# Routing logits worked out inside the second cross attention, weighing from rows turned back, and a gather-scatter program one slot shallower

## Chip, cores, metric

The kernel runs on one core of one Trainium2 chip. The metric is the device time of one execution in microseconds (us), given as the median of several runs.

## The reference, cut to what matters

Six sublayers work on x, 2 x 1024 tokens of 256 values. The change lies at the seam between the last two:

```python
# second cross attention (16 heads of 16, 64 context positions, a mask), post-norm
x = _layernorm(x + _L1_xattn_ref(x, ctx, ctx, mask, Wk, bk, Wv, bv, Wo, bo))
# experts, post-norm around them
xn = (x - mean(x)) * rsqrt(var(x) + 1e-5) * gamma + beta      # a second normalisation, with gain and offset
logits = clip(xn @ router_w.T, -1e4, 1e4)                     # 2048 x 8
probs = softmax(logits);  top 2 of the 8 experts per token, with their probabilities as gates
out = sum over the two experts of  (silu(g) * u) @ down.T,    g, u = split((gate * xn) @ gate_up.T)
x = _layernorm(x + (x + out))
```

So the router reads a layer norm (with gamma and beta) of a value that is itself a layer norm (without them), and what the experts read is xn times the gate.

## The kernel before, in words

Tokens are cut into TILES = 16 tiles of P = 128 rows. `core.x_nat` holds x by rows (128 x 16 x 256), `core.x_tr` holds it transposed (features on the partitions). PSUM is eight banks: `ps_s` and `ps_e` are two each, `ps_q`, `ps_c`, `ps_ct` and `ps_y` one each; `ps_ct` is idle in the cross attention.

**Stages.** `decoder` runs the sublayers as stages. Each is an `nc.Block()` with one program for each engine, written out in order by hand; semaphores join them, and a stage begins when every engine has left the one before. `core.stage()` then clears its semaphores.

**The second cross attention** (`stage_cross_attention`, `cross_attention`). A software pipeline over tiles: in step s an engine works on tile s (queries), s-1 (scores), s-2 (exponential and row sums), s-3 (weights, transposed), s-4 (mixing, output product, residual, moments) and s-5 (normalised row written). CROSS_LAGS = 5, so there are 21 steps. In one step TensorE does, in this order: mask and scores (L846, L854), mixing (L868), queries (L879), output product (L886), transposes of the weights (L893). ScalarE does the exponential (L902), `mixed_tr` (L907), the queries' bias (L913), the normalised row `x_nat` (L917), `e_tr` (L925). GpSimd multiplies by 1/sum (L822), turns the variance into rstd and offset (L826, L828, L830) and adds x and bias (L833). VectorE takes the maxima, subtracts, sums (L932 to L942) and makes z and its moments (L947 to L952). The sync engine (SP) starts the loads of the experts' weights (`following.load`).

**The experts' front** (first part of `stage_experts`). VectorE takes moments of all 16 tiles of x_nat (L2508, L2511), GpSimd rstd (L2297), VectorE subtracts, scales and multiplies by the gamma row (L2519, L2522), GpSimd adds the beta row into `xn`, which lies in x_tr's room (L2302). TensorE transposes xn two tiles at a time (L2354), ScalarE copies that out of PSUM (L2442), TensorE makes the logits (L2363). Then VectorE alone works out softmax, the two picks, each token's slot and the expert of each slot tile (L2529 to L2605). Meanwhile ScalarE has written 2x into `doubled` (L2431), which SP stores as the sums' start value `summed_rows` (L2252, L2254); once the gates are there ScalarE writes gate times xn for both picks (L2453, 32 of them), which SP stores as `gated_rows` (L2259), and GpSimd waits for that store and for the source index before it gathers.

**The split of the down weights.** fp32 products are made of three rounded ones, so every expert's down matrix is split: the high part by ScalarE (L2434, `split_high`), the low part by VectorE (L2236, `split_low`). Before, ScalarE does four in the front and four after `gated_written`; VectorE does four in the front and two in each of the first two steps of the loop.

**The experts' loop.** 39 slot tiles, software-pipelined by `lagged(engine, count, depth, step)`: in turn g GpSimd gathers tile g (L2218) and scatters, adding into `summed_rows`, a tile of some turns ago (L2321). Before, that is tile g-4. TensorE: hidden transposes (L2392), gate-up product (L2402), row transposes (L2409), down product (L2420), in that order, the down product two tiles behind. ScalarE copies the output out (L2492). A scatter waits until the one before it has landed. The last part loads the sums, normalises and stores.

```python
if g is not None and not at(g, 0):
    need(pool, rows_tr_ready, g - 1); pool.wait_ge(gathered, 16 * g); fetch(pool, g, turn)
if u3 is not None:
    pool.wait_ge(down_copied, u3 + 1); need(pool, scattered, 16 * u3)
    nc.gpsimd.indirect_dma_start(summed_rows, ..., rows_out[turn % UNROLL], None, compute_op=ALU.add)
```

Of the kernel before, what the change touches and what calls it, by code (L numbers as in the profile page):

```python
# [758 lines left out]

CROSS_LAGS = 5  # L760
# [3 lines left out]
def cross_attention(core, ctx, layer, weights, setup):  # L764
# [31 lines left out]
    var_eps, rstd, offset = (core.sb(ctx, f"{pre}_{n}", [P, 1]) for n in ("var_eps", "rstd", "offset"))  # L796
# [20 lines left out]
    def pool_step(pool, step):  # L817
# [5 lines left out]
        if u5 is not None:  # L823
            pool.wait_ge(var_ready, u5 + 1)
            need(pool, xn_ready, u5)
            nc.gpsimd.tensor_scalar(var_eps[:], mv[:, 1:2], LN_EPS, None, ALU.add).then_inc(eps_added, 1)  # L826
# [3 lines left out]
            nc.gpsimd.tensor_scalar(offset[:], mv[:, 0:1], rstd[:, 0:1], -1.0, ALU.mult, ALU.mult).then_inc(offset_ready, 1)  # L830
# [4 lines left out]
    def pe_step(pe, step):  # L835
# [37 lines left out]
        if t is not None:  # L873
# [7 lines left out]
            last.then_inc(q_ready, 1)  # L881
        if u4 is not None:
# [13 lines left out]
    def act_step(act, step):  # L896
# [18 lines left out]
        if u5 is not None:  # L915
            act.wait_ge(offset_ready, u5 + 1)
            nc.scalar.activation(x_nat[:, u5, :], z[:], ACT.Identity, bias=offset[:, 0:1],  # L917
                                 scale=rstd[:, 0:1]).then_inc(xn_ready, 1)
        if u3 is not None:
# [39 lines left out]
def stage_cross_attention(core, layer, weights, setup, following):  # L959

    nc = core.nc
    with core.stage() as ctx:
        cross = cross_attention(core, ctx, layer, weights, setup)
        with nc.Block() as block:

            @block.sync
            def _(sp):
                following.load(sp)

            @block.gpsimd  # L970
            def _(pool):
                for step in range(CROSS_STEPS):
                    cross.pool_step(pool, step)

            @block.tensor
            def _(pe):
                for step in range(CROSS_STEPS):
# [3 lines left out]
            def _(act):  # L981
                for step in range(CROSS_STEPS):
# [3 lines left out]
            def _(dve):  # L986
                setup.dve_keys(dve)
                setup.dve_values(dve)
                for step in range(CROSS_STEPS):
# [1105 lines left out]
def stage_experts(core, weights):  # L2095
# [9 lines left out]
    xn = core.x_tr[:].rearrange("p k (h d) -> p (k h) d", d=D)  # L2105
# [5 lines left out]
    BATCHED = BANK // D  # L2111
# [5 lines left out]
    with core.stage() as ctx:  # L2117
        scratch = core.shared[:].rearrange("p (t d) -> p t d", d=D)
        router = core.sb(ctx, "ex_router", [P, KD, EXPERTS])
# [30 lines left out]
        gamma_row, beta_row = (core.sb(front_ctx, f"ex_{n}_row", [P, D]) for n in ("gamma", "beta"))  # L2150
# [3 lines left out]
        xn_tr = [core.sb(front_ctx, f"ex_xn_tr{i}", [P, BATCHED, KD, P]) for i in range(2)]  # L2154
# [7 lines left out]
        KEPT = EXPERTS // 2  # L2162
# [589 lines left out]
```

## Time and profile before

| | us |
|---|---|
| median of 3 runs (1361.65 to 1364.32) | 1362.62 |
| the profiled execution | 1365.14 |
| its span, first to last instruction | 1363.4 |
| second cross attention, first to last TensorE instruction of it | 973.25 to 1071.65 |
| first VectorE instruction of the experts' stage | 1075.94 |
| VectorE reads the logits | 1110.27 |
| first gather issued | 1133.99 |
| last scatter issued | 1340.24 |

Times inside the trace are counted from the span's start. The rows shown further down come from the trace's views; an engine's rows give the start, the duration, the engine, the line, the operation, output<-input, and in brackets the idle time before it and what ended it. PE is TensorE's matmul side, PEld its weight load, DVE VectorE, ACT ScalarE, POOL GpSimd, SP the sync engine. PE's durations overlap one another (a matmul's end is modelled), so the distance between starts is what to read.

### The profile page before, as it was taken

What the parts mean: (1) busy time and instruction counts of PE and PEld (TensorE: products, weight loads), DVE (VectorE), ACT (ScalarE), POOL (GpSimd) and SP (SyncE); (2) the same over time, 40 slices, a digit from 0 to 9 for tenths busy, and PEclk for the clock granted to TensorE, in tenths of its full rate; (3) what the DMA queues carried; (4) which work ended last, traced back from release to release, by engine and by line L of the source; (5) the groups of instructions that cost most, each with busy time, mean ns of one, the idle gap of its engine ahead of it and who ended that gap; (6) DMA issues with size and microseconds to landing.
All of it is one profiled execution on the core that took longest, in us unless ns stands there. A gap on an engine that the chain in (4) does not pass through costs nothing. (4 is left out here: it accounts for less than half of the span.)

```text
span 1363.4 us, 25768 instructions
## 1 busy us (share of the span) xinstructions
PE 1176.5 (86%) x8215; PEld 872.0 (64%) x8216; DVE 871.6 (64%) x1536; ACT 789.9 (58%) x2129; POOL 599.9 (44%) x618
## 2 busy tenths in 40 slices
PE   7888589677799999999989999999799356999991
PEld 3544367455566777777666677767577254888881
DVE  2488789874245555566345556666588687888883
ACT  2488547423556655566455556665266355777773
POOL 1155437646454421530353232210166524888873
PEclk9999889887699999999999999999999756999996
DMA  9100000000110000000110000100460221333334
GB/s 300 44 1 1 0 1 1 1 16 16 28 36 17 16 17 16 17 17 1 32 32 16 17 1 17 47 1 2 163 209 1 74 92 55 53 54 55 55 50 135
DMA packets 42138, 58.29 MB, mean 43 GB/s; under 512 B 6608, under 2 KB 34640, under 8 KB 42032
## 3 DMA queue, kind: packets, MB, share of 16 engines
q1 hardware_dynamic: 34544, 46.70, 11.4%
q0 software_dynamic: 7488, 10.23, 4.7%
q8 instruction: 60, 0.98, 0.3%
q14 instruction: 46, 0.38, 0.1%
HBM read 32.80 MB, written 13.63 MB: 34 GB/s over the span
## 5 line engine op out<-in xcount | busy, mean ns | idle before, releaser
L2021 DVE TENSOR_REDUCE ga_neg_top<-ps 128x1 f32<-128x128 f32 (+7 forms) x256 | 182.0, 752 | 194.5 <-PE ps L1791 194.1
L1911 ACT COPY ga_e_tr<-ps 128x512 f32<-128x512 f32 (+3 forms) x192 | 92.1, 479 | 174.6 <-PE ps L1800 171.9
L1902 ACT ACTIVATE ga_e<-ps,ga_neg_top 128x128 f32<-128x128 f32 (+7 forms) x256 | 188.2, 743 | 7.5 <-DVE ga_neg_top L2021 6.8
L1800 PE MATMUL ps<-ident,ga_e 128*128 128x128 f32 x1152 | 165.1, 279 | 0.8 <-DVE ga_e_tr L2029 0.8
L1816 PE MATMUL ps<-ga_e_tr,ga_v 128*64 128x256 f32 x1152 | 151.7, 391 | 4.1 <-ACT ga_att L1919 4.1
L1800 PEld LDWEIGHTS ps<-ident,ga_e 128*128 128x128 f32 x1152 | 123.3, 142 | 28.0 <-ACT ga_e L1902 14.7
L2029 DVE COPY ga_e_tr<-ps 128x128 f32<-128x128 f32 (+3 forms) x192 | 105.8, 551 | 35.1 <-PE ps L1800 34.8
L2613 DVE TENSOR_TENSOR ex_w_lo<-ex_gate_up,ex_w_hi 128x1024 fp32r<-128x1024 f32 x78 | 95.5, 1225 | 35.1 <-ACT ex_w_hi L2467 32.1
L1976 POOL TENSOR_TENSOR ga_q_lo<-shared,ga_q_hi 128x1024 fp32r<-128x1024 f32 x15 | 35.5, 2369 | 174.7 <-ACT ga_q_hi L1892 174.7
L1816 PEld LDWEIGHTS ps<-ga_e_tr,ga_v 128*64 128x64 f32 x1152 | 72.4, 136 | 49.0 <-issue 23.4
L822 POOL TENSOR_TENSOR xa_e<-xa_e,xa_recip 128x1024 f32<-128x1024 f32 x32 | 60.9, 1902 | 68.7 <-DVE xa_recip L942 68.7
L2467 ACT CAST ex_w_hi<-ex_gate_up 128x1024 fp32r x78 | 81.6, 1049 | 15.6 <-issue 13.0
L1788 PE MATMUL ps<-ga_k_hi,ga_q_hi 64*128 64x512 f32 (+3 forms) x384 | 79.3, 409 | 4.1 <-PEq L162 2.3
L497 ACT ACTIVATE ca_e<-ps,ca_neg_top 128x64 f32<-128x64 f32 x256 | 75.9, 361 | 0.2 <-DVE ca_neg_top L528 0.2
L1962 POOL TENSOR_TENSOR shared<-shared,ga_cos 128x1024 f32<-128x1024 f32 x18 | 42.6, 2368 | 74.8 <-DMA shared<-shared 72.0
L2321 POOL DMA_INDIRECT summed_rows<-shared,ex_tile_target x39 | 62.5, 1603 | 20.7 <-issue 9.0
L1251 PE MATMUL ps<-x_tr,wide_weights 128*128 128x128 f32 x512 | 68.6, 291 | 2.0 <-ACT ga_e_tr L1911 2.0
L1251 PEld LDWEIGHTS ps<-x_tr,wide_weights 128*128 128x128 f32 x512 | 64.2, 204 | 8.2 <-issue 5.8
L1788 PE MATMUL ps<-ga_k_lo,ga_q_hi 64*128 64x512 f32 (+3 forms) x384 | 67.7, 348 | 0.0
L1788 PE MATMUL ps<-ga_k_hi,ga_q_lo 64*128 64x512 f32 (+3 forms) x384 | 67.6, 348 | 0.0
L497 ACT ACTIVATION_READ_ACCUMULATOR ca_e<-ps,ca_neg_top 128x1 f32 x256 | 65.1, 255 | 0.0
L1301 ACT ACTIVATE shared<-ps,ga_bq 128x128 f32<-128x128 f32 x128 | 36.5, 368 | 45.7 <-PE ps L1251 43.6
(335 smaller groups left out, 2830.8 us busy)
## 6 DMA issues: line engine op xcount, KB each, us to landing
shared<-shared SPq DMA_DIRECT2D x80, 128.0 KB, 2.4
ex_gate_up<-in_ex_gate_up SPq DMA_DIRECT2D x1, 8192.0 KB, 24.2
ex_down<-in_ex_down SPq DMA_DIRECT2D x1, 4096.0 KB, 35.8
x_tr<-in_x_tr SPq DMA_DIRECT2D x4, 512.0 KB, 7.0
x_nat<-in_x SPq DMA_DIRECT2D x1, 2048.0 KB, 11.4
gated_rows<-shared SPq DMA_DIRECT2D x8, 256.0 KB, 2.2
gated_rows<-x_tr SPq DMA_DIRECT2D x8, 256.0 KB, 2.3
x_tr<-summed_rows SPq DMA_DIRECT2D x8, 256.0 KB, 5.3
```

The source lines that it names most:

```text
L497: last = nc.scalar.activation(e[buffer][:, keys], ps_scores[buffer][:, keys], ACT.Exp, scale=SCALE, bias=neg_top[buffer][:, m:m + 1], accu ...
L1251: last = nc.tensor.matmul(bank[:, g * P:(g + 1) * P], wq[:, k, block_of], x_tr[:, k, J * P:(J + 1) * P], start=(k == 0), stop=(k == KD - 1))
L1788: nc.tensor.matmul(ps_scores(t, half)[:, k0:k1], qs[J % 2][rows, c * R + r, :], ks[slot][rows, c, 0:k1 - k0], start=(i == 0), stop=(i == 2 ...
L1800: last = nc.tensor.transpose(ps_tr[n % 2][:, (kb - k0) * P:(kb - k0 + 1) * P], e[half][t % 2][:, kb * P:(kb + 1) * P], core.ident[:])
L1816: last = nc.tensor.matmul(ps_att[half * HD:(half + 1) * HD, :], v[:, v_slot(b, kb), kv * HD:(kv + 1) * HD], e_tr[g % 2][:, kb, half, :], s ...
L1902: nc.scalar.activation(e[half][t % 2][:, 0:blocks(t) * P], ps_scores(t, half), ACT.Exp, bias=neg_top[t % 2][:, half:half + 1], accum_out=s ...
L1911: nc.scalar.copy(e_tr[g % 2][:, k0:k1, half, t % 2 * P:(t % 2 + 1) * P], ps_tr[n % 2][:, 0:(k1 - k0) * P].rearrange("p (k t) -> p k t", t= ...
L2021: nc.vector.tensor_reduce(neg_top[t % 2][:, half:half + 1], ps_scores(t, half), AX.X, ALU.max, negate=True).then_inc(top_ready, 1)
L2029: nc.vector.tensor_copy(e_tr[g % 2][:, k0:k1, half, t % 2 * P:(t % 2 + 1) * P], ps_tr[n % 2][:, 0:(k1 - k0) * P].rearrange("p (k t) -> p k ...
L2321: nc.gpsimd.indirect_dma_start(summed_rows, bass.IndirectOffsetOnAxis(ap=tile_target[turn % UNROLL][:], axis=0), rows_out[turn % UNROLL], ...
L2467: nc.scalar.copy(w_hi[buffer][:, k, :], weights.gate_up[:, bass.ds(x, 1), k, :] .rearrange("p a n -> p (a n)")).then_inc(w_hi_ready, 1)
L2613: nc.vector.tensor_tensor(w_lo[buffer][:, k, :], weights.gate_up[:, bass.ds(x, 1), k, :].rearrange("p a n -> p (a n)"), w_hi[buffer][:, k, ...
```

## The change

1. A new class `Router` works inside the second cross attention, which runs 23 steps in place of 21. For tile s-5, GpSimd works out a second rstd and offset beside the first (the norm of a norm: rstd of var(1+eps)+eps^2), and ScalarE writes the doubly normalised row, without gamma and beta, into `scaled`. For tile s-6 TensorE transposes it and ScalarE writes it into x_tr with gamma and beta, now one value for each partition. For tile s-7 TensorE makes the logits in `ps_ct`. The router's three small loads come ahead of the experts' weights on SP.
2. The front of the experts' stage loses its normalisation, transposes and logits. VectorE begins with the clip of the logits.
3. TensorE turns x_tr back to rows in PSUM, four tiles at a time (`turn_back`), and ScalarE weighs them from there into `scratch` (first pick) and into `doubled`'s room (second pick), in the order WEIGHED; `gated_rows` is stored in 8 pieces in place of 16.
4. ScalarE's doubling comes behind its exponential. The down weights: ScalarE splits four behind the weighing and two in each of the loop's first two steps; VectorE two before the loop (AHEAD = 2) and three in each of the first two steps.
5. GpSimd's program of the loop: depth 3 in place of 4, so turn g gathers tile g and scatters tile g-3.

```diff
+class Router:
+    def pe_step(self, pe, step):
+        u5, u6, u7 = self.tiles_of(step)
+        if u7 is not None:
+            pe.wait_ge(self.moved, u7 + 1)
...
+            for k in range(KD):
+                last = nc.tensor.matmul(self.logits[:, u7 * EXPERTS:(u7 + 1) * EXPERTS], self.xn_tr[:, k, u7 * P:(u7 + 1) * P],
+                                        self.router[:, k, :], start=(k == 0), stop=(k == KD - 1))
+            last.then_inc(self.routed, 1)
+        if u6 is not None:
+            pe.wait_ge(self.scaled_ready, u6 + 1)
+            need(pe, self.moved, u6)
+            for k in range(KD):
+                last = nc.tensor.transpose(self.ps_xn[:, k * P:(k + 1) * P], self.scaled[u6 % 2][:, k * P:(k + 1) * P], self.core.ident[:])
+            last.then_inc(self.turned, 1)
+    def act_scale(self, act, u, z, offset, rstd):
+        need(act, self.turned, u - 1)
+        return self.core.nc.scalar.activation(self.scaled[u % 2][:], z, ACT.Identity, bias=offset, scale=rstd).then_inc(self.scaled_ready, 1)
+    def act_step(self, act, step):
...
+            act.wait_ge(self.turned, u6 + 1)
+            for k in range(KD):
+                last = nc.scalar.activation(self.xn_tr[:, k, u6 * P:(u6 + 1) * P], self.ps_xn[:, k * P:(k + 1) * P], ACT.Identity,
+                                            bias=self.beta[:, k:k + 1], scale=self.gamma[:, k:k + 1])
+            last.then_inc(self.moved, 1)
...
+            if router is not None:
+                nc.gpsimd.tensor_scalar(var_eps[:, 1:2], mv[:, 1:2], 1.0 + LN_EPS, LN_EPS * LN_EPS, ALU.mult, ALU.add)
-            nc.gpsimd.tensor_tensor(rstd[:], var_eps[:], core.neg_half[:], ALU.pow).then_inc(rstd_ready, 1)
+            nc.gpsimd.tensor_tensor(rstd[:], var_eps[:], core.neg_half[:].to_broadcast([P, NORMS]), ALU.pow).then_inc(rstd_ready, 1)
...
+                def turn_back(n):
+                    if n >= 2:
+                        pe.wait_ge(gated_ready, WEIGHED.index((n - 2, 1)) + 1)
+                    for i in range(BANKED):
+                        for k in range(KD):
+                            columns = slice((n * BANKED + i) * P, (n * BANKED + i + 1) * P)
+                            last = nc.tensor.transpose(ps_xn[n % 2][:, (i * KD + k) * P:(i * KD + k + 1) * P], core.x_tr[:, k, columns], core.ident[:])
+                    last.then_inc(xn_ready, 1)
...
+                for n, i in WEIGHED:
+                    if n == 0:
+                        act.wait_ge(gates_ready, i + 1)
+                    if n == 0 and i == 1:
+                        act.wait_ge(summed_written, 16 * (TILES // DOUBLED + 1))
+                    if i == 0:
+                        act.wait_ge(xn_ready, n + 1)
+                    for j in range(BANKED):
+                        t = n * BANKED + j
+                        last = nc.scalar.activation(gated(i, t, 1).rearrange("p a d -> p (a d)"), ps_xn[n % 2][:, j * D:(j + 1) * D],
+                                                    ACT.Copy, scale=gates[:, i, t:t + 1])
+                    last.then_inc(gated_ready, 1)
+                for x in range(KEPT):
                     split_high(x)
+                act.wait_ge(gated_written, 16 * 2 * TILES // BANKED)
...
-                lagged(pool, SLOT_TILES, 4, step, turns=True)
+                lagged(pool, SLOT_TILES, 3, step, turns=True)
```

WEIGHED is (0,0), (1,0), (0,1), (1,1), (2,0), (2,1), (3,0), (3,1) as (group of four tiles, pick).

## Rows read from the trace of the kernel before

**Rows 1.** The page: shares of the chain that ended last, by engine.

```profile
DMA 7%; issue 4%; POOL 3%; DVE 1%; PE 1%; POOLq 0%; ACT 0%; DVEq 0%; ACTq 0%
```

**Rows 2.** Stretches: us, busy time of each engine (instructions), clock, DMA share, GB/s.

```profile
1000.00:1060.00 60.00, 59.02 (x525) 45.78 (x523) 52.56 (x78) 38.94 (x77) 40.06 (x55) 1.00 0.14 45
1160.00:1320.00 160.00, 160.00 (x991) 141.30 (x990) 131.02 (x166) 122.72 (x198) 131.69 (x133) 1.00 0.34 54
```

**Rows 3.** Timeline of the experts' front, VectorE.

```profile
1075.94 5.32 DVE L2508 BATCH_NORM_STATS2 ex_stats<-x_nat 128x6 f32<-128x256 f32 x16 [3.16 <-PEq L162]
...
1110.27 0.29 DVE L2529 TENSOR_SCALAR ex_logits<-ps 128x128 f32<-128x128 f32 x1 [0.43 <-PE ps L2363]
...
1112.98 0.29 DVE L2542 TENSOR_REDUCE ex_gates<-ex_probs 128x16 f32<-128x128 f32 x1
...
1132.55 0.18 DVE L2601 TENSOR_SCALAR ex_source<-ex_choice 128x40 int32<-128x40 int32 x1
```

**Rows 4.** Timeline of one steady step of the cross attention, TensorE.

```profile
1032.63 1.17 PE L846 MATMUL ps<-xa_mask_parts,xa_ident 128*128 128x512 f32 x4
...
1034.80 0.64 PE L868 MATMUL ps<-xa_e_tr,shared 128*32 128x128 f32 x16
1035.37 1.16 PE L879 MATMUL ps<-x_tr,wide_weights 128*128 128x128 f32 x8
1036.37 1.03 PE L886 MATMUL ps<-wide_weights,xa_mixed_tr 128*128 128x256 f32 x4
1037.23 1.04 PE L893 MATMUL ps<-ident,xa_e 128*128 128x128 f32 x8
1038.03 1.17 PE L846 MATMUL ps<-xa_mask_parts,xa_ident 128*128 128x512 f32 x4
```

**Rows 5.** The same step on ScalarE.

```profile
1032.48 1.08 ACT L925 COPY xa_e_tr<-ps 128x512 f32<-128x512 f32 x2 [0.19 <-PE ps L893]
1035.59 0.37 ACT L907 COPY xa_mixed_tr<-ps 128x256 f32<-128x256 f32 x1 [1.08 <-PE ps L868]
1036.57 0.63 ACT L913 ACTIVATE xa_q_tr<-ps,xa_bq 128x128 f32<-128x128 f32 x2 [0.61 <-PE ps L879]
1037.08 0.60 ACT L917 ACTIVATE x_nat<-xa_z,xa_offset,xa_rstd 128x256 f32<-128x256 f32 x1
```

**Rows 6.** The last step of the cross attention, ScalarE.

```profile
1074.15 0.60 ACT L917 ACTIVATE x_nat<-xa_z,xa_offset,xa_rstd 128x256 f32<-128x256 f32 x1 [2.74 <-POOL xa_offset L830]
```

**Rows 7.** The front: doubling, weighing, and the stores' landing (last number, us).

```profile
1077.83 1.99 ACT L2431 ACTIVATE ex_doubled<-x_nat 128x1024 f32<-128x1024 f32 x2
1119.82 6.47 ACT L2453 ACTIVATE x_tr<-x_tr,ex_gates 128x256 f32<-128x256 f32 x16
gated_rows<-x_tr SPq DMA_DIRECT2D x8, 256.0 KB, 2.3
summed_rows<-wide_weights SPq DMA_DIRECT2D x1, 128.0 KB, 4.5
```

**Rows 8.** First steps of the experts' loop, VectorE and TensorE.

```profile
1140.81 2.36 DVE L2236 TENSOR_TENSOR ex_down_rounded<-ex_down,x_rounded 128x1024 fp32r<-128x1024 f32 x2
1150.83 0.92 PE L2420 MATMUL ps<-x_rounded,shared_rounded 128*128 x4 [2.07 <-DVE shared_rounded L2619]
```

**Rows 9.** GpSimd and ScalarE around the loop's scatters: steady and last.

```profile
1236.24 1.01 POOL L2218 DMA_INDIRECT shared<-gated_rows,ex_tile_source  x1 [0.72 <-POOL ex_tile_target L2212]
1236.93 0.37 ACT L2492 COPY shared<-ps 128x256 f32<-128x256 f32 x1
1238.61 1.61 POOL L2321 DMA_INDIRECT summed_rows<-shared,ex_tile_target  x1 [0.17 <-issue]
1241.06 1.01 POOL L2218 DMA_INDIRECT shared<-gated_rows,ex_tile_source  x1 [0.65 <-POOL ex_tile_target L2212]
...
1340.24 1.57 POOL L2321 DMA_INDIRECT summed_rows<-shared,ex_tile_target  x1 [2.85 <-DMA summed_rows<-shared,ex_tile_target]
```

**Rows 10.** The chain that ended last, first piece of the loop.

```profile
1133.99 3.01 DMA shared<-gated_rows,ex_tile_source
```

More of the change, by code:

```diff
@@ L881, in pe_step @@
             last.then_inc(q_ready, 1)
+        if router is not None:
+            router.pe_step(pe, step)
         if u4 is not None:
@@ L962, in stage_cross_attention @@
     with core.stage() as ctx:
-        cross = cross_attention(core, ctx, layer, weights, setup)
+        router = Router(core, ctx)
+        cross = cross_attention(core, ctx, layer, weights, setup, router)
+        steps = TILES + Router.LAGS
         with nc.Block() as block:
@@ L971, in _ @@
             def _(pool):
-                for step in range(CROSS_STEPS):
+                for step in range(steps):
                     cross.pool_step(pool, step)
@@ L976, in _ @@
             def _(pe):
-                for step in range(CROSS_STEPS):
+                for step in range(steps):
                     cross.pe_step(pe, step)
@@ L981, in _ @@
             def _(act):
-                for step in range(CROSS_STEPS):
+                for step in range(steps):
                     cross.act_step(act, step)
@@ L988, in _ @@
                 setup.dve_values(dve)
-                for step in range(CROSS_STEPS):
+                for step in range(steps):
                     cross.dve_step(dve, step)
@@ L2104, in stage_experts @@
     nc, dram = core.nc, core.dram
-    xn = core.x_tr[:].rearrange("p k (h d) -> p (k h) d", d=D)
+    sums = core.x_tr[:].rearrange("p k (h d) -> p (k h) d", d=D)
     ROUTES = TILES * EXPERTS
@@ L2109, in stage_experts @@
     GROUP = 2
-    BATCHED = BANK // D
+    BANKED = 2 * (BANK // D)
+    WEIGHED = [(0, 0), (1, 0), (0, 1), (1, 1)] + [(n, i) for n in range(2, TILES // BANKED) for i in range(2)]
     LEFT = EXPERTS // 2
@@ L2254, in _ @@
                 sp.dma_start(summed_rows[N:N + P, :], doubled[0][:, 0, :]).then_inc(summed_written, 16)
[L2255 to L2260 removed]
+                for turn, (n, i) in enumerate(WEIGHED):
+                    tiles = slice(n * BANKED, (n + 1) * BANKED)
+                    sp.wait_ge(gated_ready, turn + 1)
+                    sp.dma_start(gated_rows[i * N:(i + 1) * N, :].rearrange("(n p) d -> p n d", p=P)[:, tiles, :],
+                                 gated(i, n * BANKED, BANKED)).then_inc(gated_written, 16)
                 sp.wait_ge(scattered, 16 * SLOT_TILES)
@@ L2308, in _, with step @@
                 fetch(pool, 0, 0)
-                def step(g, t, u1, u2, u3, turn):
+                def step(g, t, u1, u2, turn):
                     if g is not None and not at(g, 0):
@@ L2487, in step @@
                         weights_high(ahead, 0, turn % 2)
+                    if at(t, 0) or at(t, 1):
+                        first = KEPT + t * (EXPERTS - KEPT) // 2
+                        for x in range(first, first + (EXPERTS - KEPT) // 2):
+                            split_high(x)
                     if u2 is not None:
@@ L2607, in _ @@
                 dve.wait_ge(weights.loaded, 16 * weights.LOADS)
+                for x in range(AHEAD):
+                    split_low(dve, x, down_first_ready)
                 def weights_low(t, k, buffer):
@@ L2635, in step @@
                     if at(t, 0) or at(t, 1):
-                        first = KEPT + t * (EXPERTS - KEPT) // 2
-                        for x in range(first, first + (EXPERTS - KEPT) // 2):
+                        first = AHEAD + t * (EXPERTS - AHEAD) // 2
+                        for x in range(first, first + (EXPERTS - AHEAD) // 2):
                             split_low(dve, x, down_lo_ready)
```

172 lines of the change are left out of this document (66 added, 106 removed).

## The prediction

> **What bounds the kernel now.** I read the page's chain of waits first: its shares name the scatter's DMA and the issue time around it [rows 1], so the chain hardly tells what lies ahead of the loop; for that I took stretches and timelines. Stretches show three regimes. In the steady cross attention TensorE is busy 59.02 of 60 us; in the steady loop 160.00 of 160, at a granted clock of 1.00 (2.4 GHz) in both [rows 2]. Between them the experts' front is one serial line: VectorE starts at 1075.94, reads the logits only at 1110.27, and has the source index at 1132.55 [rows 3]. Call the moment at which VectorE reads the logits T; all that follows hangs on it: gates at T+3.0, sources at T+22.5, first gather at 1133.99 = T+23.7 [rows 3, 10]. Nothing overlaps that line, so what shortens it shortens the kernel, less what is put into the two TensorE-bound regimes.
>
> **1. The front's normalisation and logits go.** VectorE's first instruction of the stage becomes the read of the logits: 1110.27 - 1075.94 = -34.3 us [rows 3]. What was hidden beneath these 34 us (doubling, four splits high and low, the masks, the start values' store) has to find another cover; parts 4 and 5 charge for it.
>
> **2. TensorE in the steady cross attention.** Its groups follow each other without a gap, one step from 1032.63 to 1038.03 = 5.4 us [rows 4]. Router adds four instructions of 128x128 weights: two transposes and two products of 8 columns. Eight query products take 1036.37 - 1035.37 = 1.00 us, or 0.125 each; eight transposes 1038.03 - 1037.23 = 0.80, or 0.10 each. So 2 x 0.125 + 2 x 0.10 = 0.45 us a step. Steps 6 to 15, ten of them, are bound so (the pipeline has five lags, and queries end at step 15), the first with transposes only: 10 x 0.45 - 0.1 = +4.4 us. The new waits are met a step ahead: `scaled` and x_tr's tile are written by ScalarE in the step before. Bounds: 0 if gaps of TensorE's sequencer take them in; 10 x 1.1 = 11 if each new semaphore costs a visible gap.
> By the Trainium skill, "TensorE: Matmul & The Clock Gate", section Back-to-back issue gap, a stream of weight loads and matmuls sustains about 81 ns for each at 128 columns. The rows show 100 to 125 ns for these fp32 forms; by the page the part would be an estimated 10 x 0.32 = 3.2 us. The measured spacing stands.
>
> ScalarE gets three more a step: the scaled row, like L917's 0.60, and two copies out of PSUM, like L913's two in 0.63: 1.23 us. It stands idle 1.08 before L907, 0.61 before L913 and 0.19 before L925, 1.88 together [rows 5]. `e_tr` ended at 1033.56, and TensorE's mixing began at 1034.80 [rows 4, 5]: 1.24 of slack, plus the 0.45 by which TensorE comes later. I charge nothing. GpSimd gets one small tensor_scalar and a wider power, 0.35 us as I estimate it (0.2 for the first, 0.1 to 0.15 for the second); it stands idle by a third (40.06 busy of 60) [rows 2].
>
> **3. Two more steps at the end.** In the last steps TensorE isn't full and the order is a chain through GpSimd and ScalarE. GpSimd's +0.35 falls on it three times (tiles 13, 14, 15): +1.0. ScalarE's extra work of step 18 stands once ahead of the last `e_tr`: +1.2 at most; I take 1.1, with both copies. Then the last scaled row starts where x_nat did at 1074.15 [rows 6] and, in place of x_nat's end at 1074.75, there come: the scaled row 0.6 (x_nat now runs beside what follows), two transposes 0.3, two copies 0.7, two products 0.4, handovers 0.4 = 2.4 against 0.6, +1.8. Sum +3.9; bounds 2 and 7 (each handover doubled, clock at its lower level).
>
> **4. Doubling and weighing ahead of the gather.** ScalarE's line from T: exponential done T+1.3; doubling 4 x 0.97 [rows 7] to T+5.2; gates are there by T+3.1. Weighing is 32 x 0.405 = 13.0 (6.47 for 16 [rows 7]), read from PSUM now. The second pick must wait for the store of 2x, which is its room. Before, these stores started at 1077.6 and the last (issue to landing 4.5 us [rows 7]) was in near 1085.3, 7.7 later; now they start at T+2.4, so T+10.1. (0,0) and (1,0) are done at T+8.5: a stall of 1.6. Then (0,1) to T+11.8; TensorE turns group 2 back until T+13.8 (8 transposes at half clock, some 1.8), (1,1) done T+13.4, so 0.5 of stall; the other four groups to T+20.3. The last store is half a megabyte: landing 2.3 for 256 KB [rows 7], which I raise to 2.9; gated_written at T+23.3, against sources at T+22.5: the gather starts 0.8 later. Splits high 0 to 3 (3.9 us) hold ScalarE until T+24.2, which delays the first high weights by about the same 0.8. +0.8; bounds 0 and 4 (the start values' store twice as late as I have it).
> The Trainium skill, "DMA: Bandwidth & Descriptors", section Anatomy of one DMA, gives about 2.0 us plus bytes at 436 GB/s; an estimate from it for half a megabyte is 3.2, and the part would be +1.1. No row of before shows this size alone.
>
> **5. The splits inside the loop.** VectorE does three low splits in each of steps 0 and 1 where it did two (2.36 for two, 1.18 each [rows 8]). In both steps VectorE is what TensorE waits for: the first down product came at 1150.83 after 2.07 idle, released by VectorE [rows 8]. 2 x 1.18 = 2.4, of which 0.7 goes where VectorE itself waited for ScalarE's high weights: +1.7. Bounds 0 and 3.5 (ScalarE's four in the same steps in series too).
>
> **6. GpSimd three deep.** In the steady loop TensorE is full; GpSimd repeats every 4.82 (1236.24 to 1241.06), and a scatter starts 1.31 after ScalarE's copy (1237.30 to 1238.61) since the gather of the same turn stands ahead of it [rows 9]. With depth 3 that gather is past already: scatter 0.9 after the copy, -0.4, kept only until the scatters run one behind the other at the end, and then handed through to the last (1340.24). The gather of tile g now comes after the scatter of g-4: copy 0.37, 0.9, 2.45 to the gather (1238.61 to 1241.06), landing L, transposes and down product 2.1: 5.8 + L within two tiles, 9.64. L is 3.01 unloaded [rows 10]; in the steady loop the next gather was released by GpSimd's own copy and not by its landing, so L is below 1240.4 - 1236.24 = 4.2 [rows 9]. So -0.4; bounds -0.8 and, at L = 4.2, (10.0 - 9.64) / 2 x 36 = +6.5.
>
> **Sum.** -34.3 + 4.4 + 3.9 + 0.8 + 1.7 - 0.4 = -23.9 us. The profiled execution took 1365.14 (span 1363.4 and 1.74 around it) and becomes 1341.2; the median, 2.5 lower, becomes 1338.7.
>
> **Rivals.**
> *A. ScalarE becomes the cross attention's bound.* Its new work stands between queries and `e_tr`. If its 1.23 came in series with TensorE rather than beside it: 12.3 in place of 4.4, 1346.6. For it: the copies wait for transposes that TensorE now does after the queries. Against: the 1.88 us of idle time and the 1.24 of slack.
> *B. The gather binds the loop.* From L = 3.85 on. At 4.2: 1338.7 + 6.9 = 1345.6. Against: 3.01 in the one clear row; for: that row has no scatter beside it.
> *C. Better than summed.* TensorE's 0.45 vanishes in gaps and the first steps' splits are covered by waits: 1338.7 - 4.4 - 1.7 = 1332.6.
> *D. Slower than before.* One mechanism: in turn g the gather of the next tile stands behind a scatter that itself waits for the landing of the one before, and TensorE waits for the gather. The loop then closes on GpSimd. It costs all 23.9 us from 23.9 / 36 = 0.66 a tile, that is L = 3.85 + 2 x 0.66 = 5.2, above the 4.2 that the trace allows, unless the new order makes the two DMAs collide. 1364 and more.
> *E. The logits don't come earlier as said*, since the weighing hides none of the stores: the start values' store late by 4 more, 1342.7.
>
> **Chances.** Forecast (1335 to 1342) 0.52; A 0.16; B 0.08; C 0.12; E 0.08; D 0.03; 0.01 for no change. 0.2% of the time, 2.7 us, is about what a measurement tells from none. Faster 0.96, same 0.01, slower 0.03. The range runs from C's neighbourhood to beyond A: 1332 to 1349.
>
> **What would show it.** VectorE's read of the logits at 1075.9 + 8.3 = 1084 to 1085; steady steps of the cross attention 5.85 in place of 5.4, TensorE without gaps; ScalarE's last weighing 20.3 after the logits; first gather 24.5 after them; first down product 43 after them (40.6 before); 4.8 a tile in the loop, and the scatter 0.9 behind the copy. Wrong would be: VectorE's read later than 1090, steady steps of 6.5 or more, TensorE waiting for a gather in the loop, or a first gather more than 28 after the logits.

## The result and the profile after

The changed kernel takes 1348.32 us in the median of four runs (1348.17 to 1351.78), the kernel before 1363.47 in the runs beside it (1361.65 to 1364.44): a ratio of 0.9897, 95% interval 0.9877 to 0.9916. Faster by 15.2 us, where 23.9 was forecast. The time lies inside the range given (1332 to 1349), but 9.6 above the forecast itself and outside the 1335 to 1342 around it.

Both traces cut at the same events give the sum term by term. The events are the first VectorE instruction of the second cross attention, its fifth and its sixteenth row maximum (the last one), VectorE's read of the logits (T), the first gather, and the first down product and last scatter of the loop. All are starts, in us.

| stretch | before | after | difference | forecast |
|---|---|---|---|---|
| first VectorE instruction to fifth maximum | 23.86 | 23.83 | 0.0 | 0 |
| fifth to sixteenth maximum | 59.33 | 65.19 | +5.9 | +4.4 (part 2) |
| sixteenth maximum to T, without the 34.33 of the old front | 19.42 | 30.79 | +11.4 | +3.9 (part 3) |
| the old front | 34.33 | 0 | -34.3 | -34.3 (part 1) |
| T to first gather | 23.72 | 26.14 | +2.4 | +0.8 (part 4) |
| first gather to first down product | 16.84 | 18.50 | +1.7 | +1.7 (part 5) |
| first down product to last scatter | 189.41 | 189.72 | +0.3 | -0.4 (part 6) |
| last scatter to the end | 23.16 | 22.71 | -0.5 | 0 |
| sum | 390.07 | 376.88 | -13.2 | -23.9 |

The spans differ by 16.8 (1363.4 and 1346.6): the stretch began at 973.33 before and at 969.72 after. Nothing ahead of it was changed, and over the fourteen traces of this study it began anywhere from 969.72 to 973.93, so 3.6 of the 16.8 is no gain of the change.

The regimes of [rows 2], the same stretches of the kernel after:

```profile
1000.00:1060.00 60.00, 60.00 (x540) 48.18 (x540) 47.37 (x71) 45.97 (x100) 40.64 (x61) 1.00 0.11 33
1160.00:1320.00 160.00, 158.30 (x975) 138.96 (x974) 124.94 (x158) 117.85 (x191) 104.59 (x127) 1.00 0.33 52
```

The cross attention is TensorE's still. In the loop TensorE is not quite full any more: 158.30 in place of 160.00, and 975 instructions in place of 991.

VectorE's timeline of the front, where [rows 3] stood: the logits, the first gates, the sources.

```profile
1089.53 0.29 DVE L2561 TENSOR_SCALAR ex_logits<-ps 128x128 f32<-128x128 f32 x1 [8.31 <-PEq L162]
...
1092.25 0.29 DVE L2574 TENSOR_REDUCE ex_gates<-ex_probs 128x16 f32<-128x128 f32 x1
...
1111.82 0.18 DVE L2633 TENSOR_SCALAR ex_source<-ex_choice 128x40 int32<-128x40 int32 x1
```

From T to the sources it is 22.29, as before (22.28). T itself is 1089.53, and 1084 to 1085 was forecast.

One steady step of the cross attention on TensorE, for [rows 4]:

```profile
1032.35 1.18 PE L912 MATMUL ps<-xa_mask_parts,xa_ident 128*128 128x512 f32 x4
...
1035.09 1.16 PE L945 MATMUL ps<-x_tr,wide_weights 128*128 128x128 f32 x8
1036.09 0.51 PE L794 MATMUL ps<-ro_router,x_tr 128*128 128x8 f32 x4
1036.45 0.42 PE L801 MATMUL ps<-ident,ro_scaled 128*128 128x128 f32 x2
1036.71 1.03 PE L954 MATMUL ps<-wide_weights,xa_mixed_tr 128*128 128x256 f32 x4
```

The router's share is 1036.71 - 1036.09 = 0.62: the products 0.36 as *four* instructions, the transposes 0.26 as two.

ScalarE in the same step, for [rows 5]:

```profile
1030.78 0.60 ACT L807 ACTIVATE ro_scaled<-xa_z,xa_offset,xa_rstd 128x256 f32<-128x256 f32 x1
1031.27 0.59 ACT L987 ACTIVATE x_nat<-xa_z,xa_offset,xa_rstd 128x256 f32<-128x256 f32 x1
1031.77 0.80 ACT L817 ACTIVATE x_tr<-ps,ro_beta,ro_gamma 128x128 f32<-128x128 f32 x2
1032.45 1.07 ACT L997 COPY xa_e_tr<-ps 128x512 f32<-128x512 f32 x2
```

`e_tr` starts at 1032.45 and is needed by the mixing at 1034.52: here the new work is covered, as argued. Rival A, which ended at 1346.6, is not what happened: no steady step took 6.5, they took 6.02 where 5.85 was forecast.

The last steps on TensorE:

```profile
1065.35 1.04 PE L961 MATMUL ps<-ident,xa_e 128*128 128x128 f32 x8
1069.18 1.08 PE L934 MATMUL ps<-xa_e_tr,shared 128*32 128x128 f32 x16 [2.80 <-ACT xa_e_tr L997]
...
1071.53 1.91 PE L954 MATMUL ps<-wide_weights,xa_mixed_tr 128*128 128x256 f32 x4
1073.24 1.92 PE L961 MATMUL ps<-ident,xa_e 128*128 128x128 f32 x8
...
1084.83 1.02 PE L794 MATMUL ps<-ro_router,x_tr 128*128 128x8 f32 x4 [3.57 <-ACT x_tr L817]
```

and the same time in stretches (TensorE's busy time first, the granted clock third from the end):

```profile
1066.00:1069.00 3.00, 0.39 (x4) 0.14 (x2) 1.03 (x3) 2.61 (x6) 2.83 (x4) 1.00 0.00 0
1069.00:1070.00 1.00, 0.82 (x16) 0.60 (x16) 0.00 (x0) 0.13 (x1) 0.85 (x3) 0.56 0.00 0
1070.00:1072.00 2.00, 2.00 (x16) 1.72 (x9) 0.00 (x0) 1.58 (x4) 1.21 (x3) 0.50 0.03 8
```

TensorE waited 2.80 for ScalarE's `e_tr`. As that wait ended the granted clock went from 1.00 to 0.50 (2.4 to 1.2 GHz), and it was 0.50 until the router's end. The output product (L954) shows what that costs: 1.71 from start to start, where a steady step has 0.86. The kernel before had a wait at the same place, a shorter one:

```profile
1065.36 0.64 PE L868 MATMUL ps<-xa_e_tr,shared 128*32 128x128 f32 x16 [1.82 <-ACT xa_e_tr L925]
```

Its clock was 1.00 up to 1076, behind the end of this stage.

The stores of T to the first gather. Columns as above, DMA share and GB/s last:

```profile
1093.00:1095.00 2.00, 0.17 (x1) 0.00 (x0) 1.70 (x6) 1.91 (x3) 0.00 (x0) 0.99 1.02 341
...
1099.00:1101.00 2.00, 0.00 (x0) 0.00 (x0) 1.77 (x7) 1.15 (x4) 0.00 (x0) 0.50 1.02 340
...
1111.00:1113.00 2.00, 0.00 (x0) 0.00 (x0) 1.83 (x9) 2.00 (x3) 0.00 (x0) 0.50 0.56 206
```

The landing of the stores, for [rows 7], and ScalarE's stall in the weighing:

```profile
gated_rows<-shared SPq DMA_DIRECT2D x4, 512.0 KB, 4.5
```
```profile
1099.85 3.02 ACT L2505 ACTIVATE wide_weights<-ps,ex_gates 128x256 f32<-128x256 f32 x8 [2.14 <-DMA summed_rows<-wide_weights]
```

GpSimd at the end of them, where the first gather of [rows 10] stood:

```profile
1113.73 1.00 POOL L2286 COPY ex_tile_source<-ex_source 128x1 int32<-128x1 int32 x1 [22.90 <-DMA gated_rows<-ex_doubled]
1115.67 1.24 POOL L2295 DMA_INDIRECT shared<-gated_rows,ex_tile_source  x1 [0.94 <-POOL ex_tile_source L2286]
```

and at the same time the issue of the last store, and VectorE's two low splits ahead of the loop:

```profile
1109.44 0.36 SPq L2332 DMA_DIRECT2D gated_rows<-ex_doubled  x1
```
```profile
1112.33 2.35 DVE L2313 TENSOR_TENSOR ex_down_rounded<-ex_down,x_rounded 128x1024 fp32r<-128x1024 f32 x2
```

From the first store (1093) the 16 DMA engines are taken, at some 340 GB/s, but for one gap. The sources are there at 1111.82, and what GpSimd waits for until 1113.73 is the last store. Then its copy of one column takes 1.00, where the same copy took 0.18 in the kernel before (at 1132.87). It ends at 1114.73, 0.05 behind the second of the two splits.
By the Trainium skill, "DMA: Bandwidth & Descriptors", section Anatomy of one DMA, which is about transfers that GpSimd issues (these are SP's), bytes move at 436 GB/s. By that figure the 6.4 MB of these stores are an estimated 14.7 us. At the measured 340 GB/s they are 18.9, and the measurement decides.

The first steps of the loop, for [rows 8]: three low splits of VectorE, and the first down product.

```profile
1129.36 3.49 DVE L2313 TENSOR_TENSOR ex_down_rounded<-ex_down,x_rounded 128x1024 fp32r<-128x1024 f32 x3
```
```profile
1134.17 0.72 PE L2476 MATMUL ps<-x_rounded,shared_rounded 128*128 x4
```

GpSimd in the steady loop, for [rows 9], and after it what GpSimd waited for from 1160 to 1300 (us in total, times, longest):

```profile
1171.43 1.71 POOL L2385 DMA_INDIRECT summed_rows<-shared,ex_tile_target  x1 [1.40 <-ACT shared L2547]
1172.56 1.17 POOL L2289 COPY ex_tile_target<-ex_target 128x1 int32 x1
1173.88 1.01 POOL L2295 DMA_INDIRECT shared<-gated_rows,ex_tile_source  x1 [0.15 <-POOL ex_tile_target L2289]
```
```profile
POOL summed_rows L2385 <- ACT shared L2547: 16.0, 12, 1.5
POOL summed_rows L2385 <- DMA summed_rows<-shared,ex_tile_target: 15.1, 11, 1.6
POOL summed_rows L2385 <- DMA shared<-gated_rows,ex_tile_source: 10.2, 6, 1.7
```

ScalarE's copy of that tile ran from 1170.19 for 0.37, so the scatter starts 0.87 behind the copy's end, as forecast (0.9; before 1.31 [rows 9]).

### The profile page after: what moved, and what is told of

Its sections match the earlier page's. It is cut to its first block and busy times, and to the rows that moved or that the text cites. A ratio compares the mean times of both kernels' runs of the same rounds, so it can differ in the third digit from the quotient of the medians.

```text
span 1346.6 us, 25817 instructions
## 1 busy us (share of the span) xinstructions
PE 1181.1 (88%) x8247; PEld 874.8 (65%) x8248; DVE 845.7 (63%) x1479; ACT 802.1 (60%) x2169; POOL 567.5 (42%) x625
## 3 DMA queue, kind: packets, MB, share of 16 engines
q1 hardware_dynamic: 34672, 46.44, 11.4%
## 5 line engine op out<-in xcount | busy, mean ns | idle before, releaser
L1875 PEld LDWEIGHTS ps<-ident,ga_e 128*128 128x128 f32 x1152 | 123.3, 142 | 28.0 <-ACT ga_e L1977 14.7
```

What stands on the lines that cost most here:

```text
L1875: last = nc.tensor.transpose(ps_tr[n % 2][:, (kb - k0) * P:(kb - k0 + 1) * P], e[half][t % 2][:, kb * P:(kb + 1) * P], core.ident[:])
```

## The experiments

Each kernel starts from the changed one unless it says otherwise. "Way" is from the last maximum to T; the columns behind the ratio are from one traced execution of each kernel. Kernels with the same figure under "before" were timed beside the same runs of the kernel before. The edits are shown cut, and their comments say where a line was or went.

| kernel | median us (runs) | before | ratio, 95% | way | T to gather | gather to down | down to last scatter |
|---|---|---|---|---|---|---|---|
| e1_depth4 | 1348.76 (4) | 1362.71 | 0.9905, 0.9889 to 0.9922 | 28.91 | 26.13 | 18.04 | 188.76 |
| e2_warm | 1346.97 (4) | 1362.71 | 0.9879, 0.9859 to 0.9900 | 29.23 | 26.12 | 18.05 | 190.82 |
| e3_behind | 1346.04 (4) | 1362.71 | 0.9870, 0.9847 to 0.9894 | 26.69 | 25.69 | 18.02 | 190.25 |
| e4_warm_behind | 1345.90 (4) | 1362.71 | 0.9879, 0.9861 to 0.9896 | 25.82 | 24.99 | 18.07 | 191.21 |
| e5_twin_z | 1344.57 (4) | 1364.01 | 0.9855, 0.9839 to 0.9872 | 25.81 | 26.14 | 18.05 | 189.75 |
| e6_copies_first | 1344.73 (4) | 1364.01 | 0.9859, 0.9842 to 0.9875 | 25.21 | 26.14 | 18.01 | 189.52 |
| e7_few_start_values | 1346.03 (4) | 1364.01 | 0.9877, 0.9861 to 0.9894 | 30.82 | 23.73 | 18.28 | 189.47 |
| e8_double_first | 1346.53 (4) | 1364.01 | 0.9876, 0.9860 to 0.9893 | 28.89 | 25.00 | 18.06 | 189.58 |
| e9_joined | 1344.29 (5) | 1362.47 | 0.9870, 0.9854 to 0.9885 | 25.23 | 25.01 | 18.10 | 189.90 |
| e11_vector_weights | 1344.37 (5) | 1362.47 | 0.9869, 0.9854 to 0.9885 | 28.65 | 24.99 | 18.12 | 189.10 |
| e10_vector_weights_depth3 | 1345.53 (5) | 1362.47 | 0.9874, 0.9858 to 0.9891 | 28.64 | 25.00 | 18.11 | 190.93 |
| e12_changed_again | 1350.18 (6) | 1362.47 | 0.9908, 0.9892 to 0.9924 | 30.78 | 26.14 | 18.50 | 189.60 |

**e1_depth4: GpSimd's depth alone put back.**

```diff
-lagged(pool, SLOT_TILES, 3, step, turns=True)
+lagged(pool, SLOT_TILES, 4, step, turns=True)
```

> The changed kernel with GpSimd's program of the loop four deep again, everything else as changed. Theory: TensorE is the bound of the loop at either depth (4.85 us a tile in the changed kernel too), so the depth is worth nothing but where the last scatters stand: 1348.3 + 0.4, within 0.2%. Rival (the gather binds the shallower loop): faster by 1.5 us or more, with the time between the first down product and the last scatter shrinking from 189.7 us. Seen in the trace either way: the scatter begins 1.3 us after ScalarE's copy in place of 0.9 to 1.0.

The median is the changed kernel's, which fits the expectation and settles nothing smaller. The trace has the loop 0.96 shorter, not longer. More under e10.

**e2_warm: six unneeded transposes for TensorE in steps 17 and later.**

```diff
+if router is not None and step > TILES:
+    for _ in range(FILL):
+        nc.tensor.transpose(core.ps_q[:, 0:P], core.ident[:], core.ident[:])
```

> The changed kernel with six idle transposes of the identity into a free bank at the start of each of TensorE's steps 17 to 22 of the second cross attention. In the changed kernel the granted clock falls from 1.00 to 0.50 near 1069 us, after TensorE had stood idle at 1066 to 1069, and its groups in steps 18 to 22 take twice as long (output product 1.71 us from start to start in place of 0.87). Theory: this costs 4 to 5 us of the 7.5 that the last steps took beyond the forecast; with the clock held the kernel comes to 1344. Rival (the last steps wait for ScalarE and GpSimd, not for TensorE): 1348, since TensorE's time hides under their waits, or above for the filler.

The clock fell all the same, as the stretches around the wait show:

```profile
1066.00:1068.00 2.00, 1.41 (x13) 1.17 (x11) 0.03 (x1) 1.25 (x3) 1.90 (x4) 1.00 0.03 8
1068.00:1070.00 2.00, 0.45 (x12) 0.42 (x16) 1.01 (x3) 1.49 (x4) 1.77 (x4) 0.85 0.00 0
1070.00:1072.00 2.00, 2.00 (x19) 1.62 (x12) 0.00 (x0) 1.23 (x3) 1.59 (x3) 0.50 0.00 0
```

The filler shortened the idle stretch and did not close it. The median, 1346.97, lies between the 1344 of the theory and the rival's 1348, so nothing is shown by it on what the clock costs.

This trace has something else, in the loop: TensorE waits for a gather's landing, once.

```profile
1163.46 0.44 PE L2469 MATMUL ps<-ident,shared 128*128 128x128 f32 x2 [1.27 <-DMA shared<-gated_rows,ex_tile_source]
```

The trace of e4 has the same wait once, 1.26. Both kernels have depth 3, and both loops are over a us longer than the changed kernel's.

**e3_behind: the router's work last in each step.** TensorE's behind the transposes of the weights, ScalarE's copies behind `e_tr`.

```diff
 def pe_step / act_step:
-        router.pe_step(pe, step)      # ahead of the output product
+        router.pe_step(pe, step)      # behind the transposes of the weights
-        router.act_step(act, step)    # ahead of e_tr
+        router.act_step(act, step)    # behind e_tr
```

> The changed kernel with the router's TensorE work at the end of each step, behind the transposes of the weights, and ScalarE's two copies into x_tr behind those of e_tr. Theory: in the last steps e_tr no longer waits 0.7 us for the copies and the output product no longer 1.3 us (half clock) for the router's: 2 to 4 us, 1345; in the steady steps nothing changes (TensorE's sum is the same), still 6.0 a step. Rival (only the clock matters): within 1 us of 1348.3.

The median is 1346.04, against 1348.76 for e1 beside it. The way is 4.1 shorter, the wait for the `e_tr` in question is 1.33, and the clock stayed up behind it:

```profile
1072.07 0.65 PE L934 MATMUL ps<-xa_e_tr,shared 128*32 128x128 f32 x16 [1.33 <-ACT xa_e_tr L995]
```

```profile
1070.00:1072.00 2.00, 0.74 (x8) 0.50 (x6) 0.78 (x2) 2.00 (x5) 2.00 (x2) 1.00 0.00 0
1072.00:1074.00 2.00, 1.37 (x19) 1.05 (x20) 0.26 (x2) 1.10 (x4) 1.67 (x5) 1.00 0.00 0
...
1082.00:1084.00 2.00, 0.00 (x0) 0.00 (x0) 0.00 (x0) 1.53 (x4) 0.33 (x2) 0.73 0.00 0
```

The order of the router's work in the last steps is thus the largest single piece of the miss in part 3. The run moves TensorE's part and ScalarE's together and does not tell them apart, and the later fall of the clock is inside the 4.1 too.

**e4_warm_behind: e2 and e3 together.**

> Both: the filler of the last steps and the router's work behind. Theory: the two add, some 6 us, 1342; the read of the logits 24 us behind the last maximum of the scores in place of 31. Rival: they overlap, since with the clock up the order costs nothing: 1344.

Missed: 1345.90 and a way of 25.82, where 1342 and 24 were expected. The way is 0.9 shorter than e3's, and the clock, at 1.00 from 1082 to 1084, fell later still; the medians are the same.

**e5_twin_z: e3, and z in two buffers.**

```diff
-z = core.sb(ctx, f"{pre}_z", [P, D])
+z = [core.sb(ctx, f"{pre}_z{i}", [P, D]) for i in range(2)]
-need(dve, xn_ready, u4)
+need(dve, xn_ready, u4 - 1)
```

> The changed kernel with the router's operations behind the transposes of the weights (as e3_behind) and z in two buffers, so that VectorE's next z no longer waits for ScalarE's x_nat. Theory (the last steps are a ring: z, statistics, GpSimd's three small operations, ScalarE's scale and x_nat, next z; 4.1 to 4.3 us a turn in e3_behind with one z): the turns of the last four tiles come down to 3 to 3.5 us and the way from the last maximum to VectorE's read of the logits from 26.7 to 22.5 to 25 us; the run 1343 to 1345. Rival (TensorE's half clock or ScalarE's order sets the turns): the way stays at 26 to 27, the run 1346.

0.9 and not 2 to 4: my ring was the wrong one. A second z frees VectorE of ScalarE, and the next wait, for GpSimd, stands where the old one did, as e6's timeline shows.

**e6_copies_first: e5, and from step 19 on ScalarE's copies of the tile before come ahead of its scale.**

```diff
+if router is not None and step >= TILES + 3:
+    router.act_step(act, step)        # ahead of the scale of tile u5
```

> e5_twin_z, and in the steps from 19 on ScalarE copies the turned rows of the tile before (L817) ahead of the scale of the new one, so that TensorE's products of tile 14 are done while the last z is on its way. Theory (step 21 holds the last tile up by the wait for tile 14's copies and by its products, 1.8 to 2.3 us): 1 to 2 us less than e5_twin_z from the last maximum to the read of the logits. Rival (the last z sets it, and tile 14 is beside it): the same as e5_twin_z within 0.3 us.

0.6 on the way: the right sign, under the expected size. VectorE and GpSimd of this kernel:

```profile
1073.87 0.42 DVE L1021 TENSOR_TENSOR xa_z<-ps,xa_resid 128x256 f32<-128x256 f32 x1 [3.18 <-POOL xa_resid L899]
```
```profile
1069.46 1.90 POOL L885 TENSOR_TENSOR xa_e<-xa_e,xa_recip 128x1024 f32<-128x1024 f32 x1
1071.45 0.19 POOL L891 TENSOR_SCALAR xa_var_eps<-xa_mv 128x1 f32<-128x1 f32 x1
...
1073.05 0.73 POOL L899 TENSOR_TENSOR xa_resid<-x_nat,xa_bo_row 128x256 f32<-128x256 f32 x1
```

z waits for GpSimd's `xa_resid`, and GpSimd has no pause from 1065.18 to 1073.8: 1.90 for the weights, then four small ones and the sum, 4.28 a tile.

**e7_few_start_values: of the doubled start values only every fourth tile is stored in the front.** The other tiles get a constant, written during the cross attention, so the sums are other ones. It has 1.5 MB less to store.

> The changed kernel, but of the doubled start values only each fourth tile is stored in the experts' front (12 of 16 tiles get another value, written during the cross attention, so the sums are other ones): 1.5 MB less to store between the logits and the first gather. Theory (the stores are bound by the DMA engines, whose share is 1.00 from the first store to the last; 6.3 MB at some 340 GB/s are 18.5 us): the way from the read of the logits to the first gather falls from 26.1 us to 23.6 to 24.7, with ScalarE's stall of 2.1 us on the store of the doubled rows gone too. Rival (the last 512 KB store's own landing and the waits behind it set the gather, whatever was stored before): it stays at 25.8 to 26.3.

The first gather comes 2.4 earlier, inside the expected 23.6 to 24.7, and now GpSimd waits for the sources, not for a store:

```profile
POOL ex_tile_source L2293 <- DVE ex_source L2640: 21.3, 1, 21.3
```
```profile
1112.86 0.18 POOL L2293 COPY ex_tile_source<-ex_source 128x1 int32<-128x1 int32 x1 [21.31 <-DVE ex_source L2640]
```

So all of the 2.4 us hang on when the last store is in, but they are two pieces. GpSimd goes on 22.61 after T in place of 24.20, which is 1.6. And its copy takes 0.18 again in place of 1.00, which is 0.8: this early it stands ahead of VectorE's splits. In the twelve other traces with this front it stands beside a split and ends 0.04 to 0.05 behind it; in e2 GpSimd went on only 24.77 after T, and the first gather is still at 26.12. Nor does the run tell the bytes from ScalarE's stall, since the 2.14 went with them and the last weighing ended 2.2 earlier.

**e8_double_first: ScalarE's first doubling ahead of its exponential.**

```diff
-act.wait_ge(shifted_ready, 1); nc.scalar.activation(probs[:], logits[:], ACT.Exp)...
 for n in range(TILES // DOUBLED):
+    if n == 1:
+        act.wait_ge(shifted_ready, 1); nc.scalar.activation(probs[:], logits[:], ACT.Exp)...
```

> The changed kernel, but ScalarE's first doubling comes ahead of its Exp of the logits (ScalarE is idle for 3.3 us there). Theory (stores bound by the DMA engines from the first to the last): the first store starts some 1 us earlier, the whole row of stores with it, and the way from the read of the logits to the first gather falls from 26.1 to 25.0 to 25.4. If the doubling can't start before the block does (the end of TensorE's last product), Exp is late by up to 0.5 us, which the stores hide. Rival (the weighing or the choice of rows sets the gather): 26.0 to 26.6.

25.00, as expected in size. The stores start 1.2 earlier, but the last is in only 0.8 earlier; the copy then ends with VectorE's first split in place of the second, and the ends of the two stand 1.13 apart. So this number is VectorE's as much as the stores'.

**e9_joined: e6, e8 and depth 4.**

> The changed kernel with what the runs so far showed of use: the router's operations behind the transposes of the weights, two z, copies first in the last steps (e6_copies_first), the first doubling ahead of Exp (e8_double_first), and GpSimd's program of the loop four slots deep as before the change. Theory (the gains stand at different places of one path and add): from the last maximum to the read of the logits 25.2 us, from there to the first gather 25.0, first down product to last scatter 188.7 to 189.2; the run 1342 to 1343.5. Rival (spans shift between runs by more than these): 1344 to 1346.

Way and stores came as expected, the loop did not (189.90), and the median lies above the 1342 to 1343.5 of the theory, where the rival had it. 1344.29, against 1350.18 for the changed kernel beside it on the same chip: their intervals of the ratio (0.9854 to 0.9885, 0.9892 to 0.9924) don't overlap. This is the kernel to keep of those tried.

**e11_vector_weights: e9, and for the last two tiles VectorE multiplies the weights; GpSimd adds the bias first.**

```diff
+def on_vector(u): return router is not None and u >= TILES - 2
+if on_vector(u2):    # in dve_step, behind the reciprocal
+    nc.vector.tensor_tensor(rows, rows, recip..., ALU.mult).then_inc(weights_ready, 1)
```

> e9_joined, and for the last two tiles the multiplication of the weights by the reciprocals (L885, 1.90 us on GpSimd) is VectorE's, and from step 17 on GpSimd adds the bias to the rows ahead of its three small operations. In e6_copies_first GpSimd works without a pause from 1065.2 to 1073.7, 4.28 us a tile, and z waits for its rows. Theory (GpSimd is the bound of steps 17 to 19): the z of tiles 14 and 15 come 1.5 to 3.5 us earlier, and the way from the last maximum to the read of the logits is 22 to 23.7 instead of 25.2. Rival (the mixing, the output product and the ring of z and statistics set it anyway): 24.7 to 25.5.

Missed: the way is 28.65 in the trace, worse than e9's by 3.4, and 28.64 in the trace of e10, whose code is the same up to there. The median is e9's (1344.37 and 1344.29), though: the traced execution was the slowest of the five (1348.21, the others 1343.57 to 1345.13), with a mean granted clock of 0.940 where the others had 0.947 to 0.948. So the 3.4 are not shown for every execution. VectorE, GpSimd and TensorE at that place:

```profile
1070.47 1.23 DVE L1026 TENSOR_TENSOR xa_e<-xa_e,xa_recip 128x1024 f32<-128x1024 f32 x1
```
```profile
1070.63 1.19 POOL L902 TENSOR_SCALAR xa_offset<-xa_rstd,xa_mv 128x2 f32<-128x2 f32 x1
```
```profile
1073.96 1.08 PE L940 MATMUL ps<-xa_e_tr,shared 128*32 128x128 f32 x16 [2.67 <-ACT xa_e_tr L1003]
```

The weights did come earlier, but GpSimd's offset, 0.27 elsewhere, took 1.19, until VectorE's multiplication ended. Counted from the last maximum the offset was done at 8.95, in e9 at 7.62: 0.92 of the difference is this, the rest goes with the addition of the bias now ahead of it. ScalarE waited for the offset with `e_tr` queued behind it, TensorE waited 2.67 for `e_tr` (1.32 in e9), and with that wait the granted clock fell to 0.50 again, as in the changed kernel. Why the offset waited the Trainium skill says, "SBUF — State Buffer", section Who interferes with whom: VectorE and GpSimd share a pair of ports as an exclusive lock, and a VectorE instruction with two inputs in SBUF contends with one of GpSimd that reads SBUF. The row agrees (1.19 against 0.27).

**e10_vector_weights_depth3: e11 with depth 3.**

> e11_vector_weights, but GpSimd's program of the loop three slots deep, as in the changed kernel. Theory (the third slot's scatter stands before the next gather's landing is due and the loop loses by it): 0.5 to 1.5 us longer than e11_vector_weights, and GpSimd's waits for a gather's landing at a scatter come back. The prediction's own reading (three deep is shorter at the end by one slot's tail): 0.4 us shorter. A difference under 0.5 us in the medians would settle neither.

1345.53 against 1344.37, intervals overlapping; the trace's loop is 1.8 longer, and GpSimd's waits for a gather's landing at a scatter are back (six from 1160 to 1300, 9.9 us). What tells the depths apart is the time of 25 turns, from the fifth scatter to the thirtieth, over all traces: 121.50, 121.53, 121.62 and 121.90 in the four with depth 4 (the kernel before among them), 122.72 to 123.84 in the ten with depth 3. TensorE's row of this kernel and of e11, 1160 to 1300:

```profile
1160.00:1300.00 140.00, 139.69 (x857) 122.55 (x856) 113.34 (x144) 106.50 (x172) 95.53 (x114) 1.00 0.32 53
```
```profile
1160.00:1300.00 140.00, 140.00 (x868) 123.73 (x867) 114.54 (x145) 107.40 (x173) 115.51 (x116) 1.00 0.33 54
```

**e12_changed_again: the changed kernel once more.**

> The changed kernel once more, unchanged, beside the three on the same chip: 1346.5 to 1349.5. Its first nine operations of the change's stretch start as before; the way from the last maximum to the read of the logits, 30.8 us in one trace of this code and 28.9 in two traces with the same code at this place, shows which of the two is usual.

The median, 1350.18, is above the 1346.5 to 1349.5 expected: the same code had 1348.32 the first time, so two medians of one code can differ by 1.9. The way is 30.78, as in the first trace. In e1 and e8, whose code is the same up to T, it is 28.9: there the clock fell too, but was back at 1.00 by 1080, where here it stayed at 0.50. So the same code has two lengths, 1.9 apart.

## Why the prediction was right in its sign and wrong in its size

**Part 1** held to 0.1 us: the front's 34.3 went, and what hangs on T kept its distance to the sources.

**Part 2** (+4.4, measured +5.9) failed in the step "Router adds four instructions". An fp32 product of 128x128 weights is two instructions on TensorE here. The row said it (x8 for a line with four products), I priced one product as one of the eight, and two transposes at 0.10 each where they take 0.13. 0.62 a step in place of 0.45 is 1.7 over ten steps, all of the 1.5 missing. That TensorE binds these steps and ScalarE doesn't was right.

**Part 3** (+3.9, bounds 2 and 7, measured +11.4) is the failure that matters. The prediction added the new operations to the old chain, "once ahead of the last `e_tr`: +1.2 at most". The runs put in its place: the scaled row and the copies stood ahead of *each* `e_tr` of the last steps; TensorE waited 2.80 for one of them, where it had waited 1.82 before; the clock went to half with this wait; and TensorE's work up to T went by that clock. The bound of 7 had the lower clock in it and was passed too. e3 took 4.1 of it back by the order, of which up to 1.9 may be the clock's return or not, which differs between executions of the same code (e12 against e1 and e8); the order and the clock are not told apart further. z's single buffer and the last copies' order are 0.9 and 0.6. After all that 25.2 are left, 1.9 more than the 23.3 forecast; GpSimd's 4.28 a tile without a pause (e6) is what the trace shows there, but the one attempt to take it away (e11) ran into another wait, so that it sets the end is not shown. T itself came at 1089.53 here and at 1091.74 in e12, whose stretch began 2.3 later; the second is past the 1090 that the prediction had named as a sign of being wrong.

**Part 4** (+0.8, measured +2.4) failed in two steps. The first is the landing: 2.3 for a 256 KB store, "which I raise to 2.9", is the landing of a store that has the DMA engines to itself. Behind one another the 512 KB stores took 4.5 in the group above, and the last, issued at 1109.44, held GpSimd until 1113.73, 4.3 later. The weighing I had priced too high: it was done 19.9 after T, not 20.3. So GpSimd went on 1.6 later than in the kernel before, counted from T. The second step stood at nothing: VectorE's low splits ahead of the loop run beside GpSimd's copy of the first sources, and it took 1.00 in place of 0.18, the other 0.8. e7 takes both pieces away. How much of the landing is bytes alone stays open. Rival E did not come: the start values were in 10.3 after T, where 10.1 was forecast. (In the kernel before, the last of them was issued at 1081.10 and in 4.5 later, 1085.6 and not 1085.3; it changes nothing here.)

**Part 5** (+1.7, measured +1.7) was right in its number partly by luck. It is 18.50 in the two traces of this code and 18.0 to 18.1 in most others, which would be +1.2. In e1 and e6 TensorE waits 0.46 for VectorE ahead of the first down product, as the prediction had it; in the trace of the changed kernel it does not wait there, its own products at half clock take the time.

**Part 6** (-0.4, measured +0.3, and against depth 4 some +1.3 over 25 turns) had the scatter's time right (0.87 behind the copy) and the sign wrong: an earlier scatter does not shorten a loop that TensorE fills, and each turn is 0.05 longer. One turn of four is: in the trace after, hidden transposes start 4.85 apart but for 1169.74 to 1174.78, 5.04; in e11 the longest of four is 4.91. What makes that turn late I can't say. Of rival B, GpSimd's waits for a gather's landing are seen (6 of the turns above). TensorE waiting for a gather, the prediction's own sign of being wrong, is not in the trace of the changed kernel, but it is in two of the ten with depth 3 (e2 and e4, 1.27 and 1.26) and in none of the four with depth 4. So depth 3 costs in the loop, and B's full price of 6.9 did not come. In the medians the cost is not clear of noise.

The trace's 13.2 is thus the 23.9 less 1.5, 7.5 and 1.6 for parts 2, 3 and 4 and 0.2 for the loop with its end. The medians give 15.2; the 2.0 between are inside what the start of the stretch moves from run to run.

## What to carry to other kernels

When work is added to a software pipeline, price its steady steps and its last steps apart. In the last ones put it behind what TensorE waits for, since a wait of TensorE there can be paid twice, as a wait (2.80 here) and as the lower clock behind it. A landing time read from a lone transfer holds for a lone transfer: count the bytes that a stretch has to store, divide by the rate that the trace shows at a DMA share of 1.00 (18.9 us here), and take that as the least. To move work onto VectorE can lengthen what GpSimd does at that time, down to the copy of one column.

## What the runs showed of the hardware beyond what was expected

- Stores of 512 KB, one behind another, went at 334 to 343 GB/s with a DMA share of 0.99 to 1.02. The four from `shared` landed 4.5 us after their issue in the median; with 1.5 MB less ahead of them (e7) they landed in 3.0.
- An unchanged GpSimd operation of 2 columns took 1.19 us in place of 0.27 beside a VectorE tensor_tensor of 1024 columns (e11). A GpSimd copy of 1 column took 1.00 in place of 0.18 beside VectorE's low split, also a tensor_tensor of 1024 columns (after), and in all twelve traces with the two side by side it ended 0.04 to 0.05 behind VectorE's.
- The granted clock fell from 1.00 to 0.50 with waits of 2.80 us (after), 2.67 us (e11) and 2.14 us (e2, with the filler) in the cross attention's last steps, and not with a wait of 1.82 (the kernel before) or 1.35 (e6, where it fell some 11 us later). The same code had it back by 1080 in two traces (e1, e8) and not before T in two (after, e12), nor in e7.
